# Scale products in row-quadrant pairs around the state update, and state fades moved from GpSimd to VectorE, in a fused float32 block on one core

## What is computed

```
def step(state, inp):                      # state: (b, 16, 64, 64)
    q_t, k_t, v_t, g_t, b_t = inp
    o_t = einsum('bhd,bhde->bhe', q_t, state) * g_t
    state = A[None, :, None, None] * state + b_t[..., None, None] * (k_t[..., :, None] * v_t[..., None, :])
    return (state, o_t)
o = o * rsqrt(mean(o * o, axis=-1) + RMS_EPS) * norm_w      # per head
o = (o * gate).reshape(b, s, h * d)
return o @ Wo
```

## Time and profile before

| | us |
|---|---|
| Median of 3 runs (844.26 to 848.62) | 845.93 |
| The profiled execution | 844.06 |
| Its span, first to last instruction | 841.9 |
| TensorE (PE) busy | 796.2 (95%) |
| TensorE weight loads (PEld) busy | 690.7 (82%) |
| VectorE (DVE) busy | 548.6 (65%) |
| ScalarE (ACT) busy | 558.3 (66%) |
| GpSimd (POOL) busy | 563.2 (67%) |

### The profile page before, as it was taken

The page is one execution under the profiler, slowest core; times in us unless marked ns, Lnnn a source line. Parts: engine busy times, 40 slices in busy tenths (PEclk is TensorE's granted clock), DMA queues, the critical chain, the costliest instruction groups (busy, mean ns, idle before and its releaser), DMA issues.

```text
span 841.9 us, 31084 instructions
## 1 busy us (share of the span) xinstructions
PE 796.2 (95%) x13187; PEld 690.7 (82%) x13187; DVE 548.6 (65%) x1267; ACT 558.3 (66%) x1171; POOL 563.2 (67%) x449
## 2 busy tenths in 40 slices
PE   5879999999988999999999999999999999998897
PEld 4658999898877888888888788898888887886786
DVE  4997667685673665666656656666567566674875
ACT  4756555544778677676777767777767767665664
POOL 4971210312439889797797797977977978878361
PEclk9999999999999999999999999999999999999999
DMA  4400000100100000000000000000000000000012
GB/s 136 122 1 20 26 19 9 26 19 6 23 1 2 4 2 3 4 3 2 4 4 3 2 3 4 3 3 3 4 3 3 4 3 3 3 3 3 3 37 63
DMA packets 20423, 12.36 MB, mean 15 GB/s; under 512 B 7872, under 2 KB 19008, under 8 KB 20288
## 3 DMA queue, kind: packets, MB, share of 16 engines
q1 hardware_dynamic: 20288, 10.39, 4.4%
HBM read 8.29 MB, written 2.10 MB: 12 GB/s over the span
## 4 chain that ended last, share of the span: by engine, by line
PE 59%; POOL 4%; DVE 3%; ACT 2%; issue 2%; ACTq 0%; DVEq 0%; POOLq 0%
PE la_ps L1528 10%; PE la_ps L1530 8%; PE la_ps L1529 8%; PE la_o_ps L1591 4%; PE la_o_ps L1607 4%; PE la_s_ps L1621 4%; PE la_ps L1638 4%; PE la_ps L1572 3%; PE la_ps L1559 2%; PE la_ps L1661 2%; PE la_ps L1673 2%; PE la_ps L1675 2%; PE la_ps L1674 2%; POOL la_scale L2218 1%; ACT la_u_hi L2026 1%
## 5 line engine op out<-in xcount | busy, mean ns | idle before, releaser
L2186 POOL TENSOR_TENSOR la_coef<-la_ssk,lt_mhalf 128x32 f32<-128x32 f32 x16 | 87.1, 5442 | 68.3 <-DVE la_ssk L1855 68.3
L1528 PE MATMUL la_ps<-la_x_hi,w_hi 128*128 128x256 f32 x384 | 116.7, 304 | 2.3 <-ACT la_v L1996 1.0
L1529 PE MATMUL la_ps<-la_x_lo,w_hi 128*128 128x256 f32 x384 | 107.7, 280 | 0.0
L1530 PE MATMUL la_ps<-la_x_hi,w_lo 128*128 128x256 f32 x384 | 107.6, 280 | 0.0
L2218 POOL TENSOR_TENSOR la_scale<-la_scale,lt_mhalf 128x32 f32<-128x32 f32 x16 | 97.0, 6062 | 6.1 <-DVE la_scale L1831 6.1
L1878 DVE TENSOR_TENSOR lt_state<-la_s_ps,la_faded 128x512 f32<-128x512 f32 x62 | 42.5, 686 | 66.7 <-PE la_o_ps L1607 51.7
L1528 PEld LDWEIGHTS la_ps<-la_x_hi,w_hi 128*128 128x128 f32 x384 | 72.3, 188 | 14.1 <-issue 6.2
L531 POOL CAST w_hi<-qkv_w_raw 128x256 fp32r<-128x256 f32 x20 | 7.9, 397 | 105.1 <-PE qkv_xt_ps L577 74.7
L1529 PEld LDWEIGHTS la_ps<-la_x_lo,w_hi 128*128 128x128 f32 x384 | 72.4, 189 | 1.2 <-issue 0.8
L604 PE MATMUL qkv_v_ps<-V,qkv_probsT 128*128 128x128 f32 x544 | 72.2, 279 | 1.0 <-ACT qkv_probsT L713 1.0
L604 PEld LDWEIGHTS qkv_v_ps<-V,qkv_probsT 128*128 128x128 f32 x544 | 67.9, 192 | 5.7 <-ACT qkv_probsT L713 2.4
(11 more groups left out here) (240 smaller groups left out, 2423.8 us busy)
## 6 DMA issues: line engine op xcount, KB each, us to landing
qkv_w_raw<-in_w SPq DMA_DIRECT2D x20, 128.0 KB, 2.2
X<-in_x SPq DMA_DIRECT2D x8, 256.0 KB, 3.0
out<-X SPq DMA_DIRECT2D x8, 256.0 KB, 2.3
qkv_cos<-in_cos SPq DMA_DIRECT2D x4, 256.0 KB, 3.0
qkv_sin<-in_sin SPq DMA_DIRECT2D x4, 256.0 KB, 3.9
lt_w_out<-in_w_out SPq DMA_DIRECT2D x4, 128.0 KB, 2.7
qkv_w<-in_w_qkv SPq DMA_DIRECT2D x1, 320.0 KB, 3.5
const<-in_const SPq DMA_DIRECT2D x1, 256.5 KB, 5.1
```

Source lines behind the costliest of these rows:

```text
L1528: eng.matmul(out, l_hi, r_hi, start=True, stop=False)
L1529: eng.matmul(out, l_hi, r_lo, start=False, stop=False)
L1530: return eng.matmul(out, l_lo, r_hi, start=False, stop=True)
L2186: eng.tensor_tensor(coef[:, :], ssk[:, :], mhalf[:, :], ALU.pow).then_inc(s["coef_step"], 1)
```

## The change

- `parts` gets the 16 rounded and 16 rest scales four times, one copy in each quarter of its 128 columns, so that `scT` has them in each quarter of its rows. GpSimd's two split operations write 128 in place of 32 elements a partition.
- `spread` shrinks from 8 to 2 selectors of 128 columns; each quarter of its rows holds the selector of one j. `quadrant(j)` gives the rows: j = 0 to rows 0 to 31, 1 to 64 to 95, 2 to 32 to 63, 3 to 96 to 127. The products for one j read 32 rows, and those for j = 0 and 1, and for 2 and 3, are issued alternately into two banks.
- TensorE: turn_scales, v2 and the first pair come ahead of the update, the second pair behind it.
- VectorE: the order is scale_u 0, 1, new_state(m,0,1), fade, scale_u 2, 3; and every `fade` goes from GpSimd to VectorE, right behind the new_state whose result it reads, waiting for it. So VectorE gets one 128x512 operation more behind each of the four new_state of a step: (m-1,1,1), (m,0,0), (m,0,1), (m,1,0). In step -1 it makes the two first fades.
- ScalarE: gates g0 and g1 come ahead of square_u(m,0).
- GpSimd at the start of the phase: two memsets less, four smaller selector operations in place of two.

The products, sums and values are the same.

```diff
+def quadrant(j):
+    at = 2 * (j % 2) + j // 2
+    return slice(32 * at, 32 * (at + 1))
...
-        self.spread = sb("lt_spread", [P, NP, P], F32R)
+        self.spread = sb("lt_spread", [P, 2, P], F32R)
...
-            def spread_scales(m, j):
-                if j == 0:
+            def spread_scales(m, pair):
+
+                if pair == 0:
                     taken(eng, m, "sB")
-                bank = free(eng, m, f"b{j}")
+                jobs = (2 * pair, 2 * pair + 1)
+                banks = [free(eng, m, f"b{j}") for j in jobs]
                 for r in range(2):
-                    mm = eng.matmul(ps[bank][:, r * W:(r + 1) * W], spread[:, 2 * j + r, :], scT[:, :], start=True, stop=True)
-                mm.then_inc(full[bank], 1)
+                    for j, bank in zip(jobs, banks):
+                        rows = quadrant(j)
+                        mm = eng.matmul(ps[bank][:, r * W:(r + 1) * W], spread[rows, r, :], scT[rows, :], start=True, stop=True)
+                        if r == 1:
+                            mm.then_inc(full[bank], 1)
...
                     recall(m, 0, 1)
+                if prv:
+                    turn_scales(m)
+                if nxt:
+                    by_token(m, "v2")
+                if prv:
+                    spread_scales(m, 0)
                 if now and nxt:
                     update((m, 0, 1), (m, 1, 0))
                 elif now:
                     update((m, 1, 0))
                 if prv:
-                    turn_scales(m)
-                if nxt:
-                    by_token(m, "v2")
-                if prv:
-                    for j in range(4):
-                        spread_scales(m, j)
+                    spread_scales(m, 1)
...
                 if prv and now:
                     new_state(m - 1, 1, 1)
+                    fade(m, 1, 0)
...
                     decayed(m, 1)
                     new_state(m, 0, 0)
+                if now and nxt:
+                    fade(m, 0, 1)
+                if now:
                     guard_q(m)
                 if nxt:
                     sum_k(m + 1, 0)
+                if prv:
+                    scale_u(m, 0)
+                    scale_u(m, 1)
                 if now and nxt:
                     new_state(m, 0, 1)
+                    fade(m + 1, 0, 0)
                 if prv:
-                    for j in range(4):
-                        scale_u(m, j)
+                    scale_u(m, 2)
+                    scale_u(m, 3)
...
                 if now:
                     new_state(m, 1, 0)
+                if now and nxt:
+                    fade(m, 1, 1)
                 if nxt:
                     decayed(m + 1, 0)
...
                 if now:
+                    gates(m, "g", 0)
+                    gates(m, "g", 1)
                     square_u(m, 0)
-                    for j in range(3):
-                        gates(m, "g", j)
+                    gates(m, "g", 2)
...
-                if now and nxt:
-                    fade(m, 0, 1)
-                if now:
-                    fade(m, 1, 0)
                 if nxt:
                     decay_keys(m + 1, 0)
-                    fade(m + 1, 0, 0)
                     coefficients(m + 1)
                     weigh_v(m + 1, 0)
                     weigh_v(m + 1, 1)
-                if now and nxt:
-                    fade(m, 1, 1)
```

More of the change, by code:

```diff
@@ L1138 @@
     LOADS = 15
+    SELECTORS = 12
     def sync(self, eng):
@@ L1199, in gpsimd_selectors @@
     def gpsimd_selectors(self, eng):
-        eng.wait_ge(self.cleared, 7)
+        eng.wait_ge(self.cleared, 5)
         for r in range(2):
@@ L1207, in gpsimd_selectors @@
         eng.wait_ge(self.ones_set, 8)
[L1208 to L1211, removed]
+        for j in range(4):
+            rows, first, odd = quadrant(j), 2 * (j % 2), j // 2
+            parts = [self.const[rows, C_IDENT + at:C_IDENT + at + H].rearrange("p (i r) -> p i r", r=4)
+                     [:, first:first + 2, 2 * odd:2 * odd + 2].unsqueeze(3).broadcast_to([32, 2, 2, D]) for at in (rows.start, rows.start + H)]
+            where = self.spread[rows, :, :].rearrange("p i (h e) -> p i h e", h=2)
             eng.tensor_tensor(where, parts[0], parts[1], ALU.add).then_inc(self.ones_set, 1)
-        eng.wait_ge(self.ones_set, 10)
+        eng.wait_ge(self.ones_set, self.SELECTORS)
     def vector(self, eng):
@@ L1630, in sum_squares @@
                     if m == 0:
-                        eng.wait_ge(tables.ones_set, 10)
+                        eng.wait_ge(tables.ones_set, tables.SELECTORS)
                     eng.wait_ge(s["qsq_ready"], 2 * (m + 1))
@@ L1784, in _ @@
             ffn.values(eng, 1)
-            for j in range(4):
-                spread_scales(NT, j)
+            spread_scales(NT, 0)
+            spread_scales(NT, 1)
             ffn.keys(eng, 2)
@@ L1879, in new_state, with fade @@
                                   ALU.add).then_inc(up_read[c], 1)
+            def fade(m, b, c):
+                if c > 0:
+                    eng.wait_ge(up_read[0], B * m + b + 1)
+                elif m > 0:
+                    eng.wait_ge(up_read[1], B * (m - 1) + b + 1)
+                over_e = decay_s[:, :].unsqueeze(2).broadcast_to([P, NP, D])
+                eng.tensor_tensor(faded[:, b, :, :], state[:, b, :, :], over_e, ALU.mult).then_inc(s["faded_second" if c else "faded_first"], 1)
             def residual(m):
@@ L1955, in step @@
                     split_w_out()
+                    eng.wait_ge(tables.cleared, 5)
+                    fade(0, 0, 0)
+                    fade(0, 1, 0)
             tables.vector(eng)
@@ L2204, in decay_keys @@
                 eng.tensor_tensor(own, own, over_d(decay_k[:, :]), ALU.mult).then_inc(s["kd_ready"], 1)
[L2206 to L2212, removed]
             def invert_totals(m):
@@ L2219, in invert_totals @@
                 eng.wait_ge(s["scale_step"], 3 * m - 2)
-                high = parts[:, :, 0:H]
-                eng.tensor_tensor(high, scale[:, :, :], zeros[:, :, :], ALU.add).then_inc(s["scale_step"], 1)
+                quads = parts[:, :, :].rearrange("p b (j r) -> p b j r", j=4)
+                high = quads[:, :, :, 0:H]
+                whole, none = (ap[:, :, :].unsqueeze(2).broadcast_to([P, B, 4, H]) for ap in (scale, zeros))
+                eng.tensor_tensor(high, whole, none, ALU.add).then_inc(s["scale_step"], 1)
                 eng.wait_ge(s["scale_step"], 3 * m - 1)
-                eng.tensor_tensor(parts[:, :, H:2 * H], scale[:, :, :], high.bitcast(F32), ALU.subtract).then_inc(s["scale_step"], 1)
+                eng.tensor_tensor(quads[:, :, :, H:2 * H], whole, high.bitcast(F32), ALU.subtract).then_inc(s["scale_step"], 1)
             def step(m):
```

3 lines of the change are left out of this document (removed).

## The result

The changed kernel takes 881.85 us in the median of 4 executions (881.29 to 965.1) and the kernel before 846.82 beside it: 1.0413 times as long, 95% interval 1.0387 to 1.0439. (One execution, 965.1 us at a granted clock of 0.75, is left out of the ratio.) I had said 858.0, in 848 to 872. The direction was right, the size was not: the profiled execution lost 37.4 us where I had worked out 13.8. The profiled execution took 881.44, with a span of 879.4 against 841.9.

A forecast was written before the change was run, and what follows sets the result against it. TensorE was taken as busy nearly throughout, with chains over other engines setting some starts. +2.7 (q3), -2.1 (gates), +13.0 (fades) and +0.2 made +13.8 on 844.06: 857.9, said as 858, range 848 to 872.

The forecast's parts named there:

- VectorE is first by 0.02: At the step's end, the fade behind new_state(m,1,0) was to start at 560.20, GpSimd's second weigh_v at about 560.22.
- held behind weigh_v: Rival, chance 0.20: weigh_v starts first and holds the fade behind new_state(m,1,0); 2.5 us a step in twelve steps, 874.7 us.
- Fades at the step's end (D and A): From recall(m,1,0) past the sum of squares to turn_totals: 1.08 us a step later, less gaps, +13.0 us.
- q3 (B): Between recall(m,0,1) and project_out, the last query job starts 0.19 us later behind VectorE's scales and fade: +2.7 us.
- Gates (C): Between project_out and recall(m,1,0), gates ahead of square_u remove the fourteenth step's turn_k wait and slight delays elsewhere: -2.1 us.
- Last step: turn_scales waits there for GpSimd's longer split operations, +0.3, and the tail's pairs give back 0.1: +0.2 us.
- Start of the phase: GpSimd's clears and selectors lie before coefficients, which waits for VectorE: no cost.
- The hold's mechanism: A VectorE fade beside a wide GpSimd operation ends as if started 0.14 us before that operation's end.
- on GpSimd no fade could be held so: Said of fades left on GpSimd, against VectorE fades held by wide GpSimd operations; called the strongest point against the change.
- TensorE's own 0.8 a step: Scale products in pairs around the update would alone gain TensorE 0.8 us a step, 11.2 us in 14 steps.
- the rows pair in 0.12: Two 32-row scale products on TensorE take 0.12 us, bounds 0.12 together and 0.24 one after the other.
- the other side: Rival, chance 0.08: TensorE's gain arrives because VectorE's last scale ends early enough for v3's silu; 838.6 us, faster.

The follow-up runs named there:

- E2: The kernel before with only the four fades moved to VectorE, each behind its new_state; 873.4 us, 1.0312 times before.
- E3: The changed kernel with all four fades back on GpSimd in their old places; 847.99 us, 1.0013 times before.
- E4: The changed kernel with fade(m,1,1) later on VectorE, behind the two decayed and two gate_o; 865.02 us, 1.0230 times before.
- E8: The kernel before with the gates swap and the split order on TensorE and VectorE, keeping 128-row products and GpSimd's fades; 842.31 us, 0.9943 times before.
- E6: The kernel before with only gates g0 and g1 moved ahead of square_u(m,0); 845.74 us, 0.9985 times before.
- E5: The changed kernel with GpSimd's second weigh_v made to wait until fade(m,1,1) has run on VectorE; 868.93 us, 1.0259 times before.
- E13: The changed kernel with the update ahead of turn_scales in the last step alone; 879.42 us, 1.0399 times before.
- E9: E8 with sum_k(m+1,1) and guard_k ahead of the last two low_u, and the last step's update ahead of turn_scales; 838.4 us, 0.9908 times before.
- E1: The changed kernel with only fade(m,1,1), behind new_state(m,1,0), back on GpSimd; 866.0 us, 1.0224 times before.
- E11: E9 with one fade, fade(m,0,1), on VectorE behind new_state(m,0,0); 837.19 us, 0.9907 times before.

## Why the prediction was wrong

**The step that failed: "VectorE is first by 0.02", the order of the fade behind new_state(m,1,0) and the second weigh_v.** The rival "held behind weigh_v" was the truth, and I gave it 0.20. I had reckoned that GpSimd from guard_k on falls 0.27 back against r0. In the changed kernel weigh_v starts 0.53 ahead of r0, before it was 0.62: it fell back by 0.09. Counted from recall(m,0,1), guard_k ends 0.49 later (I had 0.39), but r0 comes 0.40 later (I had 0.12): 0.30 of it is B, from 7.82 to 8.12, and 0.09 is C, where I had taken the gates' gain off. The last 0.03 of the 0.21 that I was out is that the fade starts 1.53 behind r0 and not 1.49. So 0.02 was a difference of terms each of which was uncertain by 0.1, and with an answer of 13 us on one side and 26 on the other; the middle value was not a forecast but a coin's edge. E2, in which neither the gates nor the scale products move, has weigh_v first by 0.19 as well.

Term by term, in us, the forecast and the table above:

| | forecast | measured |
|---|---|---|
| Fades at the step's end (D and A) | +13.0 | +25.6 |
| q3 (B) | +2.7 | +2.7 |
| Gates (C) | -2.1 | +0.2 |
| Last step | +0.2 | +4.2 |
| Start of the phase | 0 | +1.6 |
| Ahead of the phase, and behind the last `su` | 0 | +3.1 |
| Sum | +13.8 | +37.4 |

**The size of that rival was right.** I had 2.5 a step for it; measured 7.40 - 5.09 = 2.31. The gaps that hid part of it were more than my 3.2: 14 times 5.09 is 71.3, so the steps of before held 5.9 of them. 32.3 - 5.9 = 26.4; D grew by 26.1. The rival as a whole, 874.7, was still 7 us short: by the gates, the last step and the phase's start.

**The hold's mechanism was right.** A held fade ends 0.54 behind the end of the GpSimd operation, as if it had started 0.14 before it: the figure that I took from one gate_u of the earlier trace rows. It holds for 171 of the 172 fades of over 0.9 us in the seven kernels that have them on VectorE (0.54 or 0.55). But "on GpSimd no fade could be held so" was wrong: beside VectorE's low_u a GpSimd fade took 1.50 in E3 in place of 1.05. (The Trainium skill, SBUF — State Buffer, SBUF: two separate sides, says that the pair of ports is an exclusive lock: of a VectorE instruction with two SBUF inputs and a GpSimd instruction that reads SBUF, whichever starts first gets it for the whole instruction and the other fully blocks. The trace agrees on the order: weigh_v first by 0.19 and the fade pays 1.57, the fade first by 0.07 in E4 and decay_queries pays 0.47. On the length it doesn't quite: the fade ends 0.54 behind and not its own 0.68, and the power, in the last section, held nobody for its length.)

**Right by luck: the q3 term.** +2.7 was forecast and B grew by 2.7, but not for my reasons: a fade in the chain of the scales costs 0.72 a step as I said (7.40 in E3, 8.12 after), and the new order gives 0.4 and not the 0.53 of my reckoning, which makes 0.31 a step; but two of before's steps in seven had a B of 8.2, which I hadn't seen (in the second of them the update starts 0.90 behind recall(m,0,1) in place of 0.51, behind GpSimd's decay_keys), and in these the change loses nothing.

**Wrong: TensorE's own 0.8 a step.** E3 and E8 show 0.4. I wrote the pair as 0.26 up to the update; it takes 0.43, and the second pair loses as much. The change also makes four more changes of form a step and not three: I had left out the one from the second pair to v3. The two products of a pair start 3 ns apart, so they do run side by side, but the second round starts 0.22 behind the first, and each change of form costs some 0.1 on top. In E3 a last 0.10 is lost at q3, behind v3's silu (E8 above). That the rows pair in 0.12 was the middle of my bounds; the measured 0.22 lies at the upper one, 0.24. With 0.4 for 0.8 the rival "the other side" would have come to some 844 and not to 838.6.

**Wrong: the gates, -2.1.** +0.2. In the fourteenth step they give 1.1, as forecast with 1.4. In the 13 others g2 is read later, the scores behind it use its bank, and each step pays 0.09. I had called that "just in time".

**Missed.** The two first fades, in step -1, run on VectorE beside GpSimd's weigh_v, which takes 4.63 for its two where it took 3.77; decay_queries behind it comes later, and TensorE's wait for it grows from 0.7 to 1.4. By the first `su` it is +1.6 (E2 has 35.7 from the phase's second turn_k to it, before 34.0), where I wrote "nothing there". In the last step TensorE has too little work to cover the way over GpSimd, and I had put only +0.3 there. It took 4.2 more. The windows of that step, before and after, and of the start of the phase after (width, busy times, granted clock):

```profile
767.70:795.00 27.30, 23.49 (x493) 19.93 (x492) 19.11 (x43) 16.19 (x32) 14.24 (x12) 1.00 0.01 2
...
800.30:831.90 31.60, 27.27 (x492) 22.61 (x492) 20.26 (x44) 16.47 (x32) 13.14 (x11) 0.84 0.01 2
250.60:254.00 3.40, 3.40 (x10) 2.67 (x10) 1.28 (x3) 2.50 (x7) 1.92 (x6) 0.52 0.01 2
```

The granted clock is 1.00 before and 0.84 after: TensorE runs parts of the step at 1.2 GHz, project_out 4.6 us in place of 3.1. That is 1.5 of the 4.2, and it isn't shown to be the change's. Ahead of project_out TensorE waits 2.18 us before and 2.18 in E2, and the step's parts start at the same times up to there, within 0.02; before keeps a clock of 1.00, E2 falls to 0.50 when project_out has run for 1.2 us and needs 4.5, and E6, with the gates alone, needs 4.6. Another 1.5 is turn_totals (3.31 behind `su`, not 1.82, behind a sum of squares at the low clock and a held fade), 0.4 the longer parts, the rest the update that now stands behind turn_scales. Of the 2.5 ahead of the phase's second turn_k, 1.5 lie between its first product and its first turn_k (5.1 us in place of 3.6), with ten products at 1.2 GHz (the third window). This isn't shown to be the change's either: E4, E5, E13 and also E8 and E9 have 1.9 to 2.8 there, E1, E2, E3, E6 and E11 0.3 or less, and E11 is E9 with one fade moved.

## What to carry to other kernels

Before an elementwise operation with two SBUF tensors goes from GpSimd to VectorE, list what GpSimd will be running at that moment: if it is a wide operation that starts first, the price is that operation's rest and not 0.7 us. Where the order of the two hangs on a few hundredths, there is no middle forecast: take the two cases with their own chances, and ask which of them the uncertainties favour; here the kernel before, without any reckoning, had weigh_v first by 0.23. Put such an operation where VectorE has time, and leave the chain alone.

## What the runs showed of the hardware

- The hold goes by who starts first, and both sides pay: fades of 0.68 took 2.25, 2.53 and 2.75 behind weigh_v and decay_queries; decay_queries of 2.39 took 2.86 and low_x of 0.75 took 1.17 behind a fade.
- GpSimd's power of 128x32 holds nobody, though it takes over 6 us. In the changed kernel two gate_u, decay_queries on VectorE and others run beside it in their usual time, and it is the power that is longer: 6.34, where the power of the coefficients takes 5.44 beside VectorE instructions that read at most one SBUF tensor (and 5.82 in E9, where low_u run beside it). The rows, VectorE then GpSimd:

```profile
587.63 2.41 DVE L1883 SCALAR_TENSOR_TENSOR la_u<-la_gate,la_u 128x1024 f32<-128x1024 f32 x2
589.96 1.21 DVE L1508 TENSOR_TENSOR la_qdT<-la_qT,lt_decay_q 128x1024 f32<-128x1024 f32 x1
...
587.79 6.34 POOL L2245 TENSOR_TENSOR la_scale<-la_scale,lt_mhalf 128x32 f32<-128x32 f32 x1 [1.87 <-DVE la_scale L1844]
```

- Products of 32 rows in different row quarters start 3 ns apart, yet two rounds lie 0.22 apart, where whole products have 0.12 each. With a change of form before and behind each, v3's last product behind the eight paired products comes 0.12 us earlier than behind eight whole ones (4.22 against 4.34 behind recall(m,0,1)).
- The same wait can end at either clock: behind an idle time of 2.18 us ahead of project_out TensorE went on at a granted clock of 1.00 in the kernel before and fell to 0.50 in E2.
